# Two cross-attention layers in one kernel: start and end of the queues rebuilt, results a slot later, the first split of transposed y moved a sample ahead

## What is computed

```
layer 0: q = Wq y + bq, k = Wk y + bk, v = Wv x + bv     (8 heads of 32 channels)
         attn = softmax(q k^T / 16)                      (32 x 32 per head, summed over all 2048 columns)
         o = Wo (attn v) + bo + x;  x1 = (o - mean) * rsqrt(var + eps) * gn_w + gn_b   (over the whole sample)
layer 1: q, k, v = W_in y + b_in; in chunks of 64 columns and per head: softmax(q^T k / sqrt(32)) with a key mask, times v
         u = (W_out att + b_out) * mask;  z = x1 + u;  out = (z - mean) * rsqrt(var + eps)   (over the columns of a channel)
```

## Time and profile before

| | us |
|---|---|
| median of 3 runs (lowest, highest) | 1660.42 (1659.11, 1662.01) |
| profiled execution, its own time | 1660.06 |
| its span | 1658.2 |
| TensorE busy | 1564.0 (94%) |
| VectorE busy | 1335.9 (81%) |
| ScalarE busy | 989.7 (60%) |
| GpSimd busy | 470.9 (28%) |

### The profile page before, as it was taken

The page is one execution under the profiler, slowest core; times in us unless marked ns, Lnnn a source line. Parts: engine busy times, 40 slices in busy tenths (PEclk is TensorE's granted clock), DMA queues, the critical chain, the costliest instruction groups (busy, mean ns, idle before and its releaser), DMA issues.

```text
span 1658.2 us, 53782 instructions
## 1 busy us (share of the span) xinstructions
PE 1564.0 (94%) x23816; PEld 1311.1 (79%) x23816; DVE 1335.9 (81%) x2006; ACT 989.7 (60%) x1779; POOL 470.9 (28%) x293
## 2 busy tenths in 40 slices
PE   3999999999999999999999999999999999999982
PEld 3888888888888888888888888888888888888872
DVE  1777978879798887978879798887978879798883
ACT  2566576575655666576575656666576575656652
POOL 0113314142232313314142232313314142231313
PEclk9999999999999999999999999999999999999995
DMA  5223232423324233232423314233232423314021
GB/s 212 88 62 103 77 111 66 134 78 115 98 65 128 77 110 104 75 113 66 137 75 116 101 62 128 78 110 103 81 107 69 135 74 116 102 61 128 22 77 51
DMA packets 96182, 158.25 MB, mean 95 GB/s; under 512 B 5328, under 2 KB 38224, under 8 KB 95696
## 3 DMA queue, kind: packets, MB, share of 16 engines
q1 hardware_dynamic: 95952, 154.83, 30.3%
HBM read 121.25 MB, written 33.55 MB: 93 GB/s over the span
## 4 chain that ended last, share of the span: by engine, by line
PE 80%; DVE 12%; ACT 3%; issue 3%; DMA 1%; POOL 1%; SPq 0%; DVEq 0%; POOLq 0%; ACTq 0%
PE pj_ps L278 38%; PE l_ps L278 11%; PE l_ps L382 6%; PE w_ps L313 6%; PE s_ps L302 6%; PE w_ps L331 5%; DVE o_sb L813 2%; PE s_ps L291 2%; PE l_ps L398 2%; PE l_ps L418 2%; ACT o_sb L570 1%; DVE row_max L691 1%; ACT y_hi L521 1%; DVE yt_hl L677 1%; DVE prob L698 1%
## 5 line engine op out<-in xcount | busy, mean ns | idle before, releaser
L895 POOL TENSOR_TENSOR prob<-prob,row_inv 128x1024 f32<-128x1024 f32 x128 | 259.8, 2030 | 980.1 <-DVE row_inv L708 980.1
L580 ACT CAST att_hi<-w_ps 128x256 fp32r<-128x256 f32 x256 | 82.6, 376 | 254.0 <-PE w_ps L331 249.8
L278 PE MATMUL pj_ps<-y_hi,w_hi 128*128 128x512 f32 x512 | 208.5, 407 | 3.7 <-DVE y_lo L673 3.7
L278 PE MATMUL pj_ps<-y_lo,w_hi 128*128 128x512 f32 x512 | 202.5, 395 | 0.0
L278 PE MATMUL pj_ps<-y_hi,w_lo 128*128 128x512 f32 x512 | 202.3, 395 | 0.0
L691 DVE TENSOR_REDUCE row_max<-s_ps 128x16 f32<-128x1024 f32 x128 | 156.0, 1218 | 47.3 <-PE s_ps L302 46.2
L703 DVE TENSOR_REDUCE row_sum<-prob 128x16 f32<-128x1024 f32 x128 | 154.9, 1210 | 45.5 <-ACT prob L562 45.5
L557 ACT COPY prob_t<-w_ps 128x512 f32<-128x512 f32 x256 | 149.8, 585 | 39.3 <-PE w_ps L313 35.7
L313 PE MATMUL w_ps<-cst,prob 128*128 128x128 f32 x1024 | 147.7, 275 | 19.9 <-DVE att_lo L715 19.1
L912 POOL TENSOR_TENSOR o_sb<-o_sb,u_sb 128x1024 f32<-128x1024 f32 x64 | 165.8, 2612 | 1.6 <-ACT o_sb L570 1.6
L698 DVE TENSOR_TENSOR prob<-s_ps,row_max 128x1024 f32<-128x1024 f32 x128 | 155.5, 1215 | 0.1
(11 more groups left out here) (105 smaller groups left out, 3576.0 us busy)
## 6 DMA issues: line engine op xcount, KB each, us to landing
y_raw<-in_ctx SPq DMA_DIRECT2D x64, 512.0 KB, 4.9
yt_raw<-in_ctx_t SPq DMA_DIRECT2D x64, 512.0 KB, 4.1
x_raw<-in_x SPq DMA_DIRECT2D x64, 512.0 KB, 4.8
out_z<-o_sb SPq DMA_DIRECT2D x64, 512.0 KB, 3.4
mask_b<-in_mask SPq DMA_DIRECT2D x64, 256.0 KB, 3.8
u_sb<-in_w SPq DMA_DIRECT2D x1, 2048.0 KB, 10.7
w_sb<-in_w SPq DMA_DIRECT2D x1, 1024.0 KB, 13.7
cst<-in_consts SPq DMA_DIRECT2D x1, 512.0 KB, 5.3
```

The lines of the kernel that those rows point to most:

```text
L278: last = mm(dst, lhs, rhs, start=i == 0, stop=i == len(todo) - 1)
L895: nc.gpsimd.tensor_tensor(cut, cut, row_inv[:, u % 2, :].unsqueeze(2).to_broadcast([P, 2 * HEADS, CHUNK]), ALU.mult).then_inc(probs_done, 1)
```

## The change

- Head: the layer 1 weights come as two transfers (query and key; value and output) without the zeros, the first of them as the very first transfer; weights_in becomes five semaphores, and each step waits for what it reads. Casts and projections of block 0 come first; c1's products follow them. bk_l is computed after split_yt(0, 0), which moves into the preamble.
- T_FINAL and T_STORE go from 9 to 10.
- split_yt of part 0 runs at the end of slot 15 of the sample ahead, on ScalarE and VectorE (there ahead of group_mean). In VectorE's slots split_x and split_yt go ahead of split_y.
- ScalarE's group_normed goes ahead of split_x and split_yt in odd slots (blocks 0 and 2), and stays at the end of even slots.
- Tail: group_deviation and the variance product go ahead, the second half of the last output projection goes to bank 0, the last join is made on VectorE (last_join), and statistics are taken in the order 0, 1, 3, 2.

```diff
-T_X1, T_Z, T_Z_STATS, T_STAT, T_FINAL, T_STORE = 1, 3, 4, 8, 9, 9
+T_X1, T_Z, T_Z_STATS, T_STAT, T_FINAL, T_STORE = 1, 3, 4, 8, 10, 10
@@ SP @@
+            sp.dma_start(w_raw[:, 0:W_HALF], w1[:, 0:W_HALF]).then_inc(wqk_in, 16)
             load_y(0, 0)
+            sp.dma_start(col[:, :, :], cols).then_inc(cols_in, 16)
+            sp.dma_start(w_raw[:, W_HALF:2 * W_HALF], w1[:, W_HALF:2 * W_HALF]).then_inc(wvo_in, 16)
             load_mask_b(0, 0)
-            sp.dma_start(cst[:, :], consts).then_inc(weights_in, 16)
-            sp.dma_start(col[:, :, :], cols).then_inc(weights_in, 16)
-            sp.dma_start(u_sb[:, :, :], w1).then_inc(weights_in, 16)
+            sp.dma_start(cst[:, :], consts).then_inc(consts_in, 16)
@@ TensorE @@
-            def wout(n, b, o):
+            def wout(n, b, o, bank=1):
...
-                if o == 1:
+                if bank == 0:
+                    pe.wait_ge(qkv_copied, count(n, 24, 6 * b + 5))
+                elif o == 1:
@@ gram_part @@
+                    else:
+                        pe.wait_ge(c1_done, 1)
@@ TensorE, preamble @@
-            pe.wait_ge(weights_in, 5 * 16)
...
+            pe.wait_ge(w_hi_done, 1)
+            pe.wait_ge(w_lo_done, 1)
+            for g in range(2):
+                qk(0, 0, Q_W, g)
+            for g in range(2):
+                qk(0, 0, K_W, g)
+            pe.wait_ge(w_hi_done, 2)
+            pe.wait_ge(w_lo_done, 2)
+            for m in range(2):
+                v(0, 0, m)
+            pe.wait_ge(cols_in, 16)
+            pe.wait_ge(wvo_in, 16)
...
+            pe.wait_ge(neg_done, 1)
+            pe.wait_ge(w0_in, 2 * 16)
@@ TensorE, tail @@
             values(n, UNITS - 2)
+            variance_over_partitions(n)
...
-            for o in range(HALVES):
-                wout(n, BLOCKS - 1, o)
-            variance_over_partitions(n)
+            wout(n, BLOCKS - 1, 0)
+            wout(n, BLOCKS - 1, 1, bank=0)
@@ ScalarE, preamble @@
+            act.wait_ge(wqk_in, 16)
+            copy(w_hi[:, 0:W_HALF], w_raw[:, 0:W_HALF]).then_inc(w_hi_done, 1)
             split_y(0, 0)
-            split_y(0, 1)
+            act.wait_ge(wvo_in, 16)
+            copy(w_hi[:, W_HALF:2 * W_HALF], w_raw[:, W_HALF:2 * W_HALF]).then_inc(w_hi_done, 1)
+            act.wait_ge(cols_in, 16)
             for g in range(2):
                 copy_q(0, 0, g)
+            split_y(0, 1)
...
+            split_yt(0, 0)
+            act.wait_ge(w0_in, 2 * 16)
+            nc.scalar.mul(bk_l[:, :], bk_row[:, :], float(L)).then_inc(consts_done, 1)
@@ ScalarE, body @@
+                    if e == 1 and not first and T_X1 <= s < T_X1 + BLOCKS:
+                        group_normed(n - 1, s - T_X1)
                     if S_X <= s < S_X + BLOCKS:
                         split_x(n, s - S_X)
-                    if S_SPLIT_T <= s < S_SPLIT_T + BLOCKS:
+                    if S_SPLIT_T < s < S_SPLIT_T + BLOCKS:
                         split_yt(n, s - S_SPLIT_T)
...
-                    if not first and T_X1 <= s < T_X1 + BLOCKS:
+                    if e == 0 and not first and T_X1 <= s < T_X1 + BLOCKS:
                         group_normed(n - 1, s - T_X1)
+                    if s == SLOTS - 1 and not last:
+                        split_yt(n + 1, 0)
@@ VectorE @@
+            def last_join(n):
+                dve.wait_ge(x1_done, count(n, 4, BLOCKS - 1))
+                dve.wait_ge(u_done, count(n, 8, 2 * BLOCKS - 1))
+                cut = slice((BLOCKS - 1) * BT, BLOCKS * BT)
+                tt(o_sb[:, :, cut], o_sb[:, :, cut], u_sb[:, :, cut], ALU.add).then_inc(z_tail, 1)
@@ VectorE, preamble @@
+            for i in range(2):
+                cut = slice(i * W_HALF, (i + 1) * W_HALF)
+                dve.wait_ge(w_hi_done, i + 1)
+                tt(w_lo[:, cut], w_raw[:, cut], w_hi[:, cut], ALU.subtract).then_inc(w_lo_done, 1)
+                if i == 0:
+                    split_y(0, 0)
             flags(0, 0)
...
+            split_y(0, 1)
+            split_yt(0, 0)
             dve.wait_ge(c1_ready, 1)
@@ VectorE, body @@
+                    if S_X <= s < S_X + BLOCKS:
+                        split_x(n, s - S_X)
+                    if S_SPLIT_T < s < S_SPLIT_T + BLOCKS:
+                        split_yt(n, s - S_SPLIT_T)
                     if j == 2 and not (last and b + 2 >= BLOCKS):
                         split_y(n, b + 2)
-                    if S_X <= s < S_X + BLOCKS:
-                        split_x(n, s - S_X)
-                    if S_SPLIT_T <= s < S_SPLIT_T + BLOCKS:
-                        split_yt(n, s - S_SPLIT_T)
...
+                    if s == SLOTS - 1 and not last:
+                        split_yt(n + 1, 0)
                 group_mean(n)
@@ VectorE, tail @@
+            group_deviation(n)
             att_low(n, UNITS - 2)
             branch(n, BLOCKS - 2, 1)
-            group_deviation(n)
+            group_variance(n)
             att_low(n, UNITS - 1)
-            for o in range(HALVES):
-                branch(n, BLOCKS - 1, o)
-            group_variance(n)
-            for q in range(BLOCKS):
+            branch(n, BLOCKS - 1, 0)
+            branch(n, BLOCKS - 1, 1, bank=0)
+            stats_of_z(n, 0)
+            last_join(n)
+            for q in (1, 3, 2):
                 stats_of_z(n, q)
@@ GpSimd, tail @@
-            for q in range(BLOCKS):
+            for q in range(BLOCKS - 1):
                 join(SAMPLES - 1, q)
```

More of the change, by code:

```diff
@@ L35 @@
 EPS = 1e-5
+W_HALF = 2 * HALVES * E
 NEG = -1e9
@@ L230, in store @@
                 sp.dma_start(out_d[n][:, :, q * BT:(q + 1) * BT], o_sb[:, :, q * BT:(q + 1) * BT]).then_inc(stored[q], 16)
+            w_raw = u_sb[:, :, :].rearrange("p h t -> p (h t)")
+            sp.dma_start(w_raw[:, 0:W_HALF], w1[:, 0:W_HALF]).then_inc(wqk_in, 16)
             load_y(0, 0)
+            sp.dma_start(col[:, :, :], cols).then_inc(cols_in, 16)
+            sp.dma_start(w_raw[:, W_HALF:2 * W_HALF], w1[:, W_HALF:2 * W_HALF]).then_inc(wvo_in, 16)
             load_mask_b(0, 0)
[L234 to L236 removed]
+            sp.dma_start(cst[:, :], consts).then_inc(consts_in, 16)
             load_y(0, 1)
@@ L239, in _ @@
             load_yt(0, 1)
-            sp.dma_start(w0_sb[:, :, :, :], w0).then_inc(weights_in, 16)
-            sp.dma_start(bk_row[:, :], bk0.to_broadcast([P, E])).then_inc(weights_in, 16)
+            sp.dma_start(w0_sb[:, :, :, :], w0).then_inc(w0_in, 16)
+            sp.dma_start(bk_row[:, :], bk0.to_broadcast([P, E])).then_inc(w0_in, 16)
             load_mask_b(0, 1)
@@ L370, in wout @@
                         pe.wait_ge(u_done, count(n, 8, 2 * (b - 1) + 1))
-                three_pass(pj_ps[1][:, :], [(wpair(O_W, i, o * P, P), (att_hi[:, b % 2, i, :], att_lo[:, b % 2, i, :]))
+                three_pass(pj_ps[bank][:, :], [(wpair(O_W, i, o * P, P), (att_hi[:, b % 2, i, :], att_lo[:, b % 2, i, :]))
                                             for i in range(HALVES)]).then_inc(wout_ready, 1)
@@ L442, in variance_over_partitions @@
                 mm(l0_ps[0][:, 1:2], mean_mat, o_dev[:, 1:2], start=True, stop=True).then_inc(var_ready, 1)
-            pe.wait_ge(weights_in, 5 * 16)
-            w_raw = u_sb[:, :, :].rearrange("p h t -> p (h t)")[:, 0:4 * HALVES * E].rearrange("p (w h o) -> p w h o", w=4, h=HALVES)
+            pe.wait_ge(w_hi_done, 1)
[10 more added lines that the diff above has]
+            pe.wait_ge(wvo_in, 16)
+            w_raw = u_sb[:, :, :].rearrange("p h t -> p (h t)")[:, 0:2 * W_HALF].rearrange("p (w h o) -> p w h o", w=4, h=HALVES)
             for o in range(HALVES):
@@ L606, in copy_u0 @@
                 copy(u0[:, :, :], l0_ps[1][:, :].rearrange("p (i o) -> p i o", i=HALVES)).then_inc(u0_copied, 1)
[L608 to L611, removed]
+            w_raw = u_sb[:, :, :].rearrange("p h t -> p (h t)")
+            w_hi = w1_hi[:, :, :, :].rearrange("p w h o -> p (w h o)")
+            act.wait_ge(wqk_in, 16)
+            copy(w_hi[:, 0:W_HALF], w_raw[:, 0:W_HALF]).then_inc(w_hi_done, 1)
             split_y(0, 0)
-            split_y(0, 1)
+            act.wait_ge(wvo_in, 16)
+            copy(w_hi[:, W_HALF:2 * W_HALF], w_raw[:, W_HALF:2 * W_HALF]).then_inc(w_hi_done, 1)
+            act.wait_ge(cols_in, 16)
             for g in range(2):
                 copy_q(0, 0, g)
+            split_y(0, 1)
             for g in range(2):
@@ L716, in att_low, with branch @@
                 last.then_inc(att_lo_done, 1)
-            def branch(n, b, o):
+            def branch(n, b, o, bank=1):
                 dve.wait_ge(wout_ready, count(n, 8, 2 * b + o))
-                stt(out=u_sb[:, o, (b % 4) * BT:(b % 4 + 1) * BT], in0=pj_ps[1][:, :], scalar=c1[:, o:o + 1], in1=mask_b[:, b % 4, :],
+                stt(out=u_sb[:, o, (b % 4) * BT:(b % 4 + 1) * BT], in0=pj_ps[bank][:, :], scalar=c1[:, o:o + 1], in1=mask_b[:, b % 4, :],
                     op0=ALU.add, op1=ALU.mult).then_inc(u_done, 1)
@@ L794, in stats_of_z @@
             def stats_of_z(n, q):
```

(13 more changed lines are left out.)

4 lines of the change are left out of this document (2 added, 2 removed).

## The result

The changed kernel takes 1604.48 us (median of 4 runs, 1602.51 to 1607.04) against 1660.82 (4 runs): a ratio of 0.9666, 95% interval 0.965 to 0.9682. The profiled execution took 1603.11, its span 1601.0.

The account below looks back on a forecast made before the run. TensorE's instruction stream was taken to bound the middle, with serial waits at both ends. Gains of 16.4 + 1.5 + 32.9 + 2.1 + 8.7 = 61.6 us from 1660.06 gave 1598.5 us, range 1591 to 1616.

Parts of the forecast that it names:

- the middle: First to last mean product, 15 samples: three stalls per sample removed and a little in the last sample, gain 35.0 us.
- the tail: After the last values: earlier variance and normalisations, three GpSimd joins plus last_join, results from 1641.1; gain 8.7 us, bounds 6 to 10.
- Head: Start to first scores: smaller, earlier first transfers let scores start at 21.4 instead of 37.77; gain 16.4 us.
- Rival C: Only the head disappoints: first transfers land as the slow 12.1 us, total 1604 us; chance 0.06.
- First sample: Gram parts 1 and 3 of the first sample wait less for their yt splits; gain 1.5 us.
- Stall (a): Gram part 0 idles 0.50 us a sample, its split behind group_variance; making it in the preceding slot 15 removes this.
- Rival A: VectorE owns the seam between samples: the moved split delays the mean, up to 1.2 x 15, total 1616 us; chance 0.14.
- Stall (c): Transpose idles 1.17 us a sample for att_lo, VectorE being in result(0); results in slots 10 to 13 leave 0.16.
- Rival B: The transpose's wait for att_lo stays, set by row reduction and att_hi, not result: total 1616 us; chance 0.07.
- Stall (b): Gram part 2 idles 0.42 us a sample, its split delayed by group_normed and split_y; both moves remove this.
- In slot 3 the same move delays the last split to 553.2, wanted at 554.0: Samples 1 to 15: ScalarE's earlier group_normed makes the last yt split later, but still in time for TensorE.
- Rival D: Slower than before: gn_done late by 5.0 us each sample blocks ScalarE in slot 1, eating all 61.6 us; chance 0.02.

Follow-up runs that it names:

- e5: The changed kernel with the split of part 0 in its own slot 0 again in samples 1 to 15: 1615.42 us.
- e4: The changed kernel with results and stores in slots 9 to 12 again: 1623.67 us.
- e9: e2 with VectorE's split_y ahead of split_yt again, as in the kernel before: 1606.70 us.
- e2: The changed kernel with all four of ScalarE's normalisations back at the end of their slots: 1595.90 us.
- e8: The changed kernel with GpSimd's first join of each sample waiting for VectorE's last split of yt: 1594.99 us.
- e1: The changed kernel with only the normalisation of block 2 back at the end of slot 3: 1595.21 us, and 1594.54 in a second set.
- the change again: The changed kernel run once more, unedited, as base for the follow-up runs: 1605.21 us.
- e10: e1 with twelve products that nobody reads in TensorE's three idle stretches of the tail: 1592.71 us.

## Why the prediction was right, and where it was wrong

The time (1598.5 forecast, 1604.48 measured) lies in the range, by terms of which two were off in opposite directions: the middle by 8.3 too much gain, the tail by 3.7 too little. The second is luck, since no step had priced the clock behind it. The range did not need that luck: the change's execution with the long tail took 1608.17. The range's lower bound has no sum behind it: of its 7 us the quick bounds that the prediction states give some 3 (y's landing 1.5 earlier, the tail 10 in place of 8.7).

- **Head, right.** The weights half came at 5.0 (forecast 4.8), y at 6.6 (6.8), the first projection at 9.30 (9.4) and the scores at 21.15 (21.4; 20.9 to 22.2 over all traces with this head). Rival C did not occur.
- **First sample, right.** It gained 1.5, as forecast.
- **Stall (a), right.** Its part of the table is not seen alone, but e5 takes 10.2 back for a forecast of 9.6. The seam held: bn_aggr ran from 406.51 to 406.87, and TensorE's mean product at 407.09 had no idle. Rival A did not occur.
- **Stall (c), right.** The forecast was 1.17 a sample net; e4 took back 18.5 / 15 = 1.23 by the medians and 1.05 by the middle of the traces. Rival B did not occur.
- **Stall (b), right in its cause, but the change removed it twice.** The forecast was 0.58 a sample, e9 shows 0.72. The prediction said that the split was late twice, by the normalisation and by split_y. By its own figures one was enough: 548.2 - 1.15 is 547.05, and TensorE wanted it at 547.1. e2 shows that the order of the splits suffices, so the normalisation need not have been moved at all.
- **"In slot 3 the same move delays the last split to 553.2, wanted at 554.0": the step that failed.** It priced VectorE's split as a pass that nothing meets (1.22, chained as in slot 1), and put the meeting with GpSimd's join at nothing. By the trace the cast was done 0.2 us after GpSimd had begun its first join, and VectorE was held to that join's end: 3.24 us for the pass, and 0.71 of idle at Gram part 3. At the 1.23 that it takes in e8 the pass would have ended near 429.1, 1.5 ahead of TensorE, which was free at 430.6; it ended at 431.1. e1 and e8 give back 10 us in two independent ways. The prediction had read the very rule out of the earlier trace rows, but applied it to the tail alone, and not to the slot where the change moves a cast towards a join. It had also named it from the Trainium skill ("SBUF — State Buffer", section "Terms", on the shared port pair), which says that the loser fully blocks; this trace agrees, with 3.24 us against 1.23.
- **Tail, right in its mechanism and, at equal clocks, in its size.** In the tail of before the clock was 0.66 and then 0.50, as in the change again, and between these two the gain is 39.58 - 30.61 = 9.0, against 8.7. In the first profiled execution the clock stayed at 2.4 GHz, and the gain was 12.4; by the table above the clock goes with the difference. Of the lock: last_join took 1.50 at 1585.71, and the three joins 8.02 in place of 3 x 2.31. That fits VectorE held for up to 0.4 and GpSimd's third join for 1.1. In the change again last_join came later, met only the third join, and took 1.83, while the joins took 7.04. Neither was tested by itself.
- **Rival D** did not occur: gn_done came at 412.4 and the normalisation at 412.91, with no idle at Gram parts 1 and 2.

A version that beats both kernels is e1, or e8, at 1595, and e10 at 1592.7, 4% below the kernel before. In e1 between 700 and 1500 us TensorE is busy 798.4 of 800 us, so by this profile the middle has at most some 1.6 us in 800 left for reordering.

## What to carry to other kernels

When a step is moved, look not only at whether it still comes in time for its reader, but at which long pass on the other engine it will now meet. Here VectorE and GpSimd held each other off for a whole instruction, and being 0.2 us late cost VectorE 2.0 us, most of a join's 2.3. A wait that makes the long, unhurried pass come second (e8) was then as good as moving the short one earlier (e1). And of a change in several parts, take each back alone: here one of five was a loss that the sum of the others hid.

## What the runs showed that was not expected

- The same kernel's tail took 27.22 or 30.61 us, as TensorE's granted clock stayed at 2.4 GHz or fell to 1.2 GHz after its work had thinned out; that is 3.4 of the 5.0 us between the two profiled executions. With twelve unused products, in stretches where TensorE would have stood idle, it was 1.00 throughout in the one trace taken.
- A 1.2 us pass of VectorE took 3.24 us when it came 0.2 us behind the start of a GpSimd join. It took 1.96 when it came ahead of the end of a scaling pass that was followed by that join: in the second case the waiting VectorE, not GpSimd's next instruction, came first.
